# Attention scores of sixteen heads: both score streams chunk by chunk on the two row halves of TensorE, part of the causal mask from constant operand rows

## What is computed

```python
h = x @ W1 + b1                       # (16, 512, 384), per head q, k, v of 8
w = einsum('bhqd,bhkd->bhqk', q, k) / 8 ** 0.5
w = softmax(w * tril - (1 - tril) * 1e6, axis=-1)
a = einsum('bhqk,bhkd->bhqd', w, v)
x = layernorm(x + a @ Wp + bp)
x = layernorm(x + feed_forward(x))    # token shift, sigmoid gate, relu squared
```

## Time and profile before

| | |
|---|---|
| median of 3 runs | 749.07 us (747.19 to 750.34) |
| the profiled execution | 743.35 us, span 741.6 us |
| TensorE matmuls busy | 594.5 us (80%), 7405 instructions |
| VectorE busy | 586.1 us (79%), 1515 |
| ScalarE busy | 471.1 us (64%), 918 |
| GpSimd busy | 378.1 us (51%), 520 |
| granted TensorE clock, mean | 0.973 |

### The profile page before, as it was taken

How to read it: one execution, slowest core, us unless ns; L and a number is a source line. 1 busy time by engine, 2 the same in 40 slices (tenths; PEclk the granted TensorE clock), 3 DMA queues, 4 the chain that set the end, 5 groups by cost and what they waited for, 6 DMA issues and landing times.

```text
span 741.6 us, 19206 instructions
## 1 busy us (share of the span) xinstructions
PE 594.5 (80%) x7405; PEld 284.6 (38%) x7405; DVE 586.1 (79%) x1515; ACT 471.1 (64%) x918; POOL 378.1 (51%) x520
## 2 busy tenths in 40 slices
PE   2256888898888989898988888898989898887633
PEld 1013343444343535353443444353535344443221
DVE  3067888889899898989898989989898989892431
ACT  1110677686867676777777686767677776767710
POOL 6110334465655656565546465565656554556633
PEclk9998899999999999999999999999999999999985
DMA  2231313131222324131314122242314141201100
GB/s 57 91 108 46 96 53 115 47 116 46 81 95 60 116 60 118 48 120 32 118 39 130 47 84 93 59 117 60 116 45 122 34 108 34 75 4 31 30 15 15
DMA packets 63328, 53.42 MB, mean 72 GB/s; under 512 B 8706, under 2 KB 59012, under 8 KB 63236
## 3 DMA queue, kind: packets, MB, share of 16 engines
q1 hardware_dynamic: 63236, 52.20, 24.6%
HBM read 34.87 MB, written 17.30 MB: 70 GB/s over the span
## 4 chain that ended last, share of the span: by engine, by line
PE 42%; DVE 35%; ACT 10%; issue 5%; POOL 4%; DMA 2%; SPq 1%; POOLq 0%; DVEq 0%; ACTq 0%
DVE rowmax L646 17%; PE ops L495 9%; PE sps L464 7%; PE tps L447 7%; ACT probs L576 6%; PE spare L372 5%; PE spare L380 5%; DVE h L703 4%; PE spare L386 3%; DVE rowmax L650 3%; DVE result L703 2%; DVE attn L684 2%; PE sps L471 2%; DVE qk_rest L674 2%; DVE stats L657 2%
## 5 line engine op out<-in xcount | busy, mean ns | idle before, releaser
L576 ACT ACTIVATE probs<-tps 128x512 f32<-128x512 f32 x640 | 346.4, 595 | 128.9 <-PE tps L447 127.9
L646 DVE TENSOR_REDUCE rowmax<-sps 128x1 f32<-128x512 f32 (+2 forms) x768 | 342.8, 504 | 55.1 <-PE sps L476 51.2
L750 POOL TENSOR_SCALAR_AFFINE_SELECT probs<-probs 128x512 f32<-128x512 f32 x256 | 158.0, 635 | 249.7 <-ACT probs L576 249.5
L464 PE MATMUL sps<-kop,qop 48*128 48x128 bf16 (+3 forms) x1024 | 128.1, 309 | 61.9 <-DVE rowmax L646 35.9
L495 PE MATMUL ops<-probs,vop 128*32 128x384 f32 (+3 forms) x2048 | 169.7, 437 | 5.0 <-POOL probs L750 3.2
L447 PE MATMUL tps<-qop,kop 50*128 50x384 bf16 (+3 forms) x1024 | 126.0, 304 | 27.7 <-ACT probs L576 27.0
L650 DVE TENSOR_REDUCE rowmax<-sps 128x2 f32<-128x512 f32 x128 | 82.4, 686 | 15.5 <-PE sps L476 14.6
L447 PEld LDWEIGHTS tps<-qop,kop 50*128 50x128 bf16 x1024 | 34.5, 94 | 143.4 <-ACT probs L576 109.3
L464 PEld LDWEIGHTS sps<-kop,qop 48*128 48x128 bf16 x1024 | 40.4, 95 | 117.0 <-DVE rowmax L646 70.3
L471 PE MATMUL sps<-qmask,rows_of 64*128 64x256 bf16 (+1 forms) x640 | 83.4, 257 | 0.0
L495 PEld LDWEIGHTS ops<-probs,vop 128*32 128x32 f32 x2048 | 55.2, 109 | 69.5 <-issue 52.8
(11 more groups left out here) (73 smaller groups left out, 612.1 us busy)
## 6 DMA issues: line engine op xcount, KB each, us to landing
d_parts<-qk_parts SPq DMA_DIRECT2D x16, 768.0 KB, 3.9
qop<-d_parts SPq DMA_DIRECT2D x192, 32.0 KB
qop<-d_parts SPq DMA_DIRECT2D x64, 96.0 KB
kop<-d_parts SPq DMA_DIRECT2D x192, 32.0 KB
kop<-d_parts SPq DMA_DIRECT2D x64, 96.0 KB
xa<-L_attn_x SPq DMA_DIRECT2D x16, 256.0 KB, 3.0
xres<-L_attn_x SPq DMA_DIRECT2D x16, 256.0 KB, 3.4
out<-result SPq DMA_DIRECT2D x16, 256.0 KB, 2.5
```

The costliest lines, as they stand in the source:

```text
L464: nc.tensor.matmul(sps[:, bank(n + hh), off:off + w], qop[r, par, pair, BLK * a:BLK * a + BLK], kop[r, par, pair, 0:w], start=j == 0, stop ...
L576: nc.scalar.activation(probs[:, g % 2, i, :], tps[:, bank(4 * GROUPS * n + 4 * g + i), :], ACT.Exp, scale=SCALE)\
L646: last = nc.vector.reduce_max(rowmax[:, par, QUARTET * half + t, hh, a:a + 1], sps[:, bank(n), off:off + w], axis=AX_X)
L750: last = nc.gpsimd.affine_select(out=v, in_=v, compare_op=ALU.is_ge, fill=0.0, base=0, pattern=[[0, QUARTET], [1, BLK]], channel_multiplie ...
```

## The change

- TensorE works by chunk: `scores(b, par, g, i)` writes chunk i of S and chunk i of T together, S first, with S on the row half that T does not use (`max_head` is 1 minus the head of the T chunk). Their matmuls alternate; then come the two mask matmuls of the S chunk, both on its half.
- Each chunk waits for its own bank (`bank_free(n)`), S before T.
- The mask is split in another way. Of a diagonal block, queries 0 to 63 against keys 64 to 127 are wholly masked. Four constant rows (`BLOCKS`), one per block of 128, do that in the score matmuls: in `qop` -1e30 where the query is in the first half of block a, in `kop` 1 where the key is in its second half. The two remaining quarters are triangles of 64x64, added by two mask matmuls of 64 columns per block with the same moving operand. The rows stand between the 48 terms and the two rows of maxima: 52 contraction rows for S, 54 for T.
- The rows are loaded once: an input `half_rows` (8x512), a cast on VectorE, four DMAs from SBUF into both operands in the second step of SyncE's program.
- VectorE reduces the chunk of head `max_head(c, i)` where it was `i % 2`. ScalarE and GpSimd do what they did.

```diff
-C_IDENT, C_SEL, C_MASK, C_END = 0, 128, 384, 640
+C_IDENT, C_SEL, C_MASK, C_END = 0, 128, 384, 512
...
-def pair_free(n):
-    return n + 2 - BANKS
+def bank_free(n):
+    return n + 1 - BANKS
...
+def max_head(c, i):
+    return 1 - exp_chunk(c, i)[0][1]
...
-        qmask = sb("qmask", [P, 2, P], BF16)
+        qmask = sb("qmask", [P, 2, HROWS], BF16)
+        halves_in = sb("halves_in", [2 * BLOCKS, SEQ])
+        halves = sb("halves", [2 * BLOCKS, SEQ], BF16)
...
+                (halves_in[:], half_rows),
...
+            def place_halves(operand, first):
+                for hh in range(2):
+                    r = HROWS * hh + TERMS
+                    sp.dma_start(operand[r:r + BLOCKS].rearrange("r k p n -> r (k p) n"),
+                                 halves[first:first + BLOCKS, :].unsqueeze(1).to_broadcast([BLOCKS, 2 * PAIRS, SEQ]))\
+                        .then_inc(halves_placed, 16)
...
-                    r = HROWS * hh + TERMS
+                    r = HROWS * hh + TERMS + BLOCKS
...
+                if b == FIRST_STEP + 1:
+                    sp.wait_ge(halves_cast, 1)
+                    place_halves(qop, 0)
+                    sp.wait_ge(kop_cleared, 1)
+                    place_halves(kop, BLOCKS)
...
-            def t_unit(b, par, g, i0):
-                n = 4 * GROUPS * before("T", b) + 4 * g + i0
+            def t_matmul(b, par, g, i, j):
+                n = 4 * GROUPS * before("T", b) + 4 * g + i
                 half, c = divmod(g, CHUNKS)
-                if c == 0 and i0 == 0:
-                    wait(pe, max_in[half], 32 * (before("T", b) + 1))
-                wait(pe, exp_done, pair_free(n))
-                chunks = [exp_chunk(c, i0 + k) for k in range(2)]
-                for j in range(len(chunks[0])):
-                    for k in range(2):
...
+                if j == 0:
+                    if c == 0 and i == 0:
+                        wait(pe, max_in[half], 32 * (before("T", b) + 1))
+                    wait(pe, exp_done, bank_free(n))
+                chunk = exp_chunk(c, i)
+                t, hh, a, off, w = chunk[j]
+                pair = QUARTET * half + t
+                r = slice(HROWS * hh, HROWS * hh + TERMS + BLOCKS + MROWS)
+                last = nc.tensor.matmul(tps[:, bank(n), off:off + w], kop[r, par, pair, BLK * a:BLK * a + BLK],
+                                        qop[r, par, pair, BLK * a:SEQ], start=True, stop=True)
...
-            def s_unit(b, par, g, i0):
...
+            def s_matmul(b, par, g, i, j):
+                n = 4 * GROUPS * before("S", b) + 4 * g + i
                 half, c = divmod(g, CHUNKS)
...
+                u = 2 * c + i // 2
+                hh = max_head(c, i)
+                if j == 0:
+                    if u == 0 and i == 0:
+                        wait(pe, ops_in[half], LOADED * (before("S", b) + 1))
+                        if before("S", b) == 0 and half == 0:
+                            pe.wait_ge(halves_placed, 16 * 4)
+                    wait(pe, s_reduced, bank_free(n))
...
+            def s_masks(b, g, i):
...
+                rhs = qmask[r, 0:out.shape[1], :]
+                nc.tensor.matmul(out[:, :, 0:HROWS], rows_of[r, 0, :], rhs, start=False, stop=False,
+                                 skip_group_check=True)
+                nc.tensor.matmul(out[:, :, HROWS:], rows_of[r, 1, :], rhs, start=False, stop=True,
+                                 skip_group_check=True).then_inc(s_done, 1)
+
+            def scores(b, par, g, i):
+                c = g % CHUNKS
+                for j in range(2):
+                    if active("S", b) and j < len(max_unit(2 * c + i // 2)):
+                        s_matmul(b, 1 - par, g, i, j)
+                    if active("T", b) and j < len(exp_chunk(c, i)):
+                        t_matmul(b, par, g, i, j)
+                if active("S", b):
+                    s_masks(b, g, i)
...
-                    for i0 in (0, 2):
-                        if active("T", b):
-                            t_unit(b, par, g, i0)
-                        if active("S", b):
-                            s_unit(b, 1 - par, g, i0)
-                        spare_use(b, par, g, i0 // 2)
+                    for i in range(QUARTET):
+                        scores(b, par, g, i)
+                        if i % 2 == 1:
+                            spare_use(b, par, g, i // 2)
...
+            nc.vector.tensor_copy(halves[:], halves_in[:]).then_inc(halves_cast, 1)
...
-                hh = i % 2
+                hh = max_head(c, i)
```

63 lines of the change are left out of this document (28 added, 35 removed).

## The result

The changed kernel takes **726.61 us** (median of 4 runs, 722.77 to 731.99) beside 749.71 us of the kernel before (4 runs, 747.19 to 752.48): a ratio of 0.969 with a 95% interval of 0.965 to 0.974. Forecast were 732.0 and "faster"; both the sign and the range held. Once two kinds of VectorE instruction whose length happens to change are taken out of the step, a term that the prediction costed at nothing brings nearly the whole gain of the steady part, and the term that was to bring it brings almost nothing.

What follows compares the result with a forecast made beforehand. VectorE was taken to set the pace, with idle gaps waiting for TensorE's scores. Steps -10.5, fill -5.2 and -2.0, setup +0.7 sum to -17.0 us: 726.4 profiled, forecast 732.0 against the median; 8-in-10 range 708 to 751.

Steps and rivals of the forecast that it cites:

- the term that was to bring it: S and T side by side by chunk on TensorE: S chunk ready in 0.53 us against 0.81, or 0.48 against 0.73.
- fourteen steps: Steady steps 1 to 14: each 0.75 us shorter, 39.4 instead of 40.15, together -10.5 us.
- the four groups: Score chunks behind VectorE's four larger gaps before row maxima: ready 0.28, 0.42, 0.42 and 0.69 us earlier.
- in series: Rival: mask weight loads wait for their half's matmul, shrinking the 0.28 us to 0.09; 745 to 750 us, chance 0.16.
- no overlap: Rival: S and T do not overlap on TensorE, some 1.5 us more per step; 765 us, chance 0.04.
- ScalarE did not starve: Rival: T waits behind S and ScalarE starves; +1.8 us per step, 768 us, chance 0.09.
- (3), the banks: Releasing each chunk's bank by itself: only the first chunk goes earlier, TensorE no further ahead where VectorE sets the pace.
- q and k gaps: -0.06: VectorE's gaps before `qk_rest`: the unit ahead of `spare` ends 0.06 us earlier per step, no more.
- (2), the masks at nothing: Fewer mask columns on TensorE: -0.01 to 0 us per pair, saved columns given back by the lost pairing.
- The fill: Before the steady part: -5.2 us from 39 to 76 us, -2.0 from 76 to 110, by closing VectorE's regular gaps.
- (6), the setup: Start of the kernel, the new 8x512 cast less a halved `qmask` cast: +0.7 us, between 0 and +4.
- larger gain: Rival: the early first chunk lets VectorE never starve, 3.5 us per step; 693 us, chance 0.11.

Runs made afterwards that it cites:

- f0: The changed kernel run a second time, unaltered, as the measure on the second chip: 727.44 us, ratio 0.971.
- g2: The kernel before with only GpSimd's split of the maxima moved from group 7 to group 8: 744.15 us, ratio 0.992.
- f2: The changed kernel with GpSimd's split of the maxima moved from group 7 to group 8: 722.27 us, ratio 0.962.
- g4: The changed kernel with GpSimd's split of the maxima in group 8 and T ahead of S in each chunk: 722.50 us, ratio 0.964.
- g3: The changed kernel with banks released only by pairs and GpSimd's split of the maxima in group 8: 732.94 us, ratio 0.978.
- f3: The changed kernel without the two mask matmuls of each S chunk: 727.53 us, ratio 0.970.
- e4: The kernel before, still in pairs, with the constant rows and 64-column masks: 750.08 us, ratio 1.001.
- e2: The changed kernel with the old masks (128 and 64 columns) and without the constant rows: 727.69 us, ratio 0.970.
- e1: The changed kernel, but a chunk's bank counts as free only when a pair is, as before: 737.24 us, ratio 0.983.
- e3: The kernel before with the S pair ahead of the T pair in program order: 744.76 us, ratio 0.992.

## Why the prediction was right, and where it was wrong

**Sign, size and range** held: 726.61 for 732.0, inside 708 to 751. The sum was -17.0 us; by the medians the change brings 23.1. Fill and setup were put at -6.5 and came out at -7.4 (-4.7 by the profile of f0); fourteen steps at -10.5 and came out at -15.3; the drain at 0, and it is 0 once the same clock is granted (31.35 us in g2, 31.27 in f2). That the sum came so near is in part luck: what was forecast for the steady step is there in the gaps before maxima and is lost again elsewhere, and a release that was costed at nothing stands in its place.

**The observable steps were right.** Seen from the start of k's `qk_rest` (317.54 before, 304.55 after) the four groups come 0.27, 0.51, 0.50 and 0.80 us earlier; forecast were 0.28, 0.42, 0.42 and 0.69. The ready time is 0.54 (forecast 0.53), gaps of 0.40, 0.46 and 0.45 stand where 0.3, 0.5 and 0.3 were forecast, and the 0.9 stayed. S and T overlap, and two masks on one half don't wait for each other's loads: the rivals "in series" and "no overlap" are out by the TensorE rows above. ScalarE did not starve; g4 shows that the order in a chunk does not matter.

**The step that failed is (3), the banks.** It said: "So where VectorE sets the pace TensorE gets no further ahead than now", and of the stretch from 330.6 to 353, "no edit of TensorE's order can shorten that part". In two steps:
- *The stretch without a gap was not without waits.* From the last gap's group to k's next `qk_rest` it was 27.06 us before (330.63 to 357.69) and is 26.72 now. Before, a pair was started when the chunk but one before it was reduced, and was ready some 0.6 later, just after VectorE had finished the other; it came about 0.1 too late again and again, in recorded busy time. I had looked for idle time, and there was none to see; the distance of neighbouring starts (0.61 us in a pair, 0.73 from pair to pair) would have shown it.
- *The release brings the gain.* With pair release the changed kernel has R 36.21 and 36.19, the kernel before 36.28 and 36.27: chunks side by side, with constant rows, bring **0.07 us per step**, not 0.75. With the early release it is 35.10 and 35.09: **1.10 us**. The order is still needed, since only chunks that are written one by one can be let go one by one. The release was changed for S and for T at once; which of the two brings how much was not tested. The forecast shifts of the four groups are real and present in g3 too (its gaps before maxima are 0.40, 0.46, 0.92, 0.45), but without the early release they are lost again in front of q and k (0.55 each for 0.33) and in two new small waits of 0.11 and 0.13. "q and k gaps: -0.06" had this sign wrong: they grew to 0.42 and 0.50 in the changed kernel, and in every variant with the new order their sum is larger than before (0.83 at the least, in f3, for 0.67). What makes ScalarE's part late there I have not tried to find, beyond that it isn't S standing first (g4).

**(2), the masks at nothing,** was right for this order, with the reason that it gave: in pairs the shorter masks bring 0.45 of R (e4), in chunks 0.17 (e2), so most is given back by the lost pairing. That in pairs the clock takes it all back (e4) was no part of it. The masks in 64-column pieces last no longer, 213 ns as before.

**The fill** was right in size and reason: the shorter ready time takes its gap from 0.42 to 0.31 (e1), the first chunk written ahead takes the rest. By the first add, 125.6 in f2 and 131.1 in g3, the release is worth some 5.5 us of it. That is a rough figure: it rests on one profile of each, the fill varies by 2 to 3 us, and in g3 the clock fell to half for 3.4 us at 126.8, in f2 not.

**(6), the setup,** was +1.2 (41.18 for 40.02) where +0.7 was forecast; the cast of 8x512 takes 0.75.

**The rival "larger gain"** took it that the early first chunk lets VectorE never starve. It has the right agent, and the wrong place: the gaps behind `gate` and PV are still there, as the forecast said.

Not settled: whether the step's "luck" with `h` and `result` could be had on purpose. With all eight at 341 ns the changed kernel's step would be R + 2.73, 37.8 to 37.9 us, by this sum (35.10 + 2.73); no kernel with the early release got there.

One small slip: by its own rows (360.8 of 400 us busy, steps of 40.15) the floor that the prediction gives as 36.1 us is 36.2; nothing hangs on it.

## What to carry to other kernels

Where two engines pass tiles to and fro, look at the distance between starts and not only at idle time: a consumer that gets each second tile a tenth of a microsecond late can be booked as fully busy, and freeing a buffer one tile earlier can be worth more than getting the tile ready faster (here 1.10 us of R against 0.07). When an edit shifts the order in time, first take out what happens to collide or not (here eight VectorE instructions per step that lengthen beside GpSimd), or a chance hit will be taken for the edit's effect, as in e1 and e3. And price less work on TensorE only after a look at its granted clock.

## What the hardware did that I had not expected

- **VectorE's `tensor_scalar` beside GpSimd.** `h` of 128x128 takes 334 to 345 ns undisturbed and up to 1164 when GpSimd is at work on SBUF; a one-group move of two small GpSimd instructions (0.29 and 0.42 us) is worth 0.5 us per step in both kernels. By the Trainium skill (SBUF — State Buffer, Who interferes with whom) `tensor_scalar` can run in a mode that takes the port pair shared with GpSimd, and the one that comes second is blocked for the other's whole instruction, while `tensor_reduce` never contends on this chip. The traces agree in part: `h` and `result` vary from kernel to kernel, and in the changed kernel 21 maxima of 512 columns beside GpSimd's masks take 677 to 681 ns where 144 others take 671 to 693. Which one has to wait is less plain: three of the four `h` shown above also run beside a GpSimd instruction, and take 336 to 341 ns.
- **The clock can fall when mask columns are taken out.** The granted clock is full throughout 200 to 600 us in twelve of the fourteen profiles and falls to half in e4 and f3. TensorE's busy time does not tell them apart: 350.3 and 346.5 us of the 400 in these two, but 347.5 and 349.5 in e1 and g3, where nothing falls. The changed kernel has the masks of e4, and no fall. In the 3 us from 337 to 340, just ahead of the fall at 341 in e4, TensorE was busy for 1.68 us, and it is so at this place in every step of e4, most of them without a fall.
- **It falls in the drain as well,** at 680.9 us in the changed kernel and in the profiled execution before only at 715.8: 4.4 us of difference between two profiles that no edit made.
